# Side-by-side 16-bit one-hots and ranks from column counts in a four-layer graph network kernel

## The chip, the cores and the metric

One core of a Trainium2 chip runs the whole program. The metric is the time on the device in microseconds (us), the median of three runs. The engines are PE (matrix products; its weight loads are listed as PEld), DVE (vector), ACT (scalar, activations), POOL (GpSimd) and SP (which here only issues transfers).

## What is computed

Four graph layers over 6250 nodes with 256 features and 106250 edges, each followed by a sum with its input and a layer norm. The edges are sorted by destination; every undirected edge is there in both directions, and every node has a loop.

```python
edge_index = jnp.stack([src, dst])
x = _layernorm(x + _L0_gnn_ref(x, edge_index, weight, attn_l, attn_r))   # 4-head attention on two rows
x = _layernorm(x + _L1_gnn_ref(x, W, edge_index))                 # segment_sum of h[src] * norm
x = _layernorm(x + _L2_gnn_ref(x, edge_index, w, W1, b1, W2, b2))  # two weighted passes, relu
x = _layernorm(x + _L3_gnn_ref(x, W, edge_index))                 # segment_sum over src of h[dst]
```

A layer is a product with a weight matrix and then a sum over edges of scaled rows of the source node into the destination node.

## The kernel before

**Tiling.** Nodes are 49 blocks of 128 (`NBK`); the feature row of a node lies along one partition. The edges of a destination block fill at most 18 columns (`NC`) of 128, called chunks: 49 x 18 = 882 in all (`NK`). For each chunk POOL gathers the 128 source rows from a table in memory into one of seven tiles `G` (L2062, an indirect transfer; the tile is free when the matmul seven chunks earlier is done, L2061), DVE writes a one-hot of the destination within the block (`M`, L1266, from `dlo`), and PE multiplies both and sums into one bank (L1968).

**Stages.** A first stage does layer 0. Pass 1 (882 chunks) sums the edges of layer 1. Passes 2 and 3 sum those of layer 2, but there only 522 and 486 chunks are gathered; the other blocks are dense products with prepared matrices of edge weights (`AW`, L1927). Layer 4 at the end (L1941, L1999) is dense throughout, with prepared matrices of edge counts (`AT`). Layer 4's degrees are counted in pass 2 with trains of one-hots on DVE (`degrees`, L1286 and L1288).

**What is built behind pass 1.** The matrices `AT` and `AW` are made block by block while pass 1 runs, in spare time of the engines. `build_steps` gives each step a due chunk, 17 chunks (`PITCH`) per block, and `aggregate` on every engine runs its steps of chunk k after its own part of chunk k; within a chunk the steps of earlier blocks come first. Each engine's queue is in order, with semaphores between them. For a block i, in the order of `BORDER`:
- `cellhot` (DVE, L1321 to L1326): `OH`, for each edge a one-hot over 26 places of the pair of source blocks it comes from (a "cell"), 26 x 18 per partition.
- `rank` (PE, L1849 to L1861), in three parts: how many earlier edges share the cell. One matmul with a strictly lower triangle counts earlier partitions of the same column, and 17 matmuls with `onesb` add each column to all later ones.
- `pick`, `pack`, `over`, `less`, `slots` (DVE, L1327 to L1347): read the rank of each edge from bank `PR`, 0 to 127 within a place (an overflow place takes the rest), into `slots`.
- `load` (DVE, L1348): `OHP` = `OH` times the payload of the edge (source within the pair, destination, and for the 22 weighted blocks three pieces of the weight). This is one TENSOR_TENSOR (L1356), with another for weighted blocks (L1355).
- `place` (DVE, L1357): `S`, for each of the 18 columns a one-hot of the slot, one TENSOR_SCALAR of 128 elements each. `permute` (PE, L1862): 18 matmuls of `S` and `OHP` put every edge's payload in its slot. `cells` (ACT, L1625) copies the bank to `clf` (32 bit) and `clb` (16 bit).
- `pairhot` (DVE, L1362), 13 batches of two places a block, 637 in all: `doh`, the one-hot of the destination, one TENSOR_TENSOR for two places with the two values side by side in the last dimension (L1373); `soh`, the one-hot of the source among 256, one TENSOR_SCALAR a place (L1375); for the 286 batches of weighted blocks `wdoh`, `doh` times two weight pieces (L1379). `third` (ACT) writes the third piece.
- `pair` and `weigh` (PE, L1868 to L1893) multiply the one-hots into banks that ACT copies out (`keep`, `keepw`) and SP stores.

The lines that matter most on DVE and PE:

```python
# pairhot, L1373 to L1376
done(e.tensor_tensor(doh[n_ % NB][:, :, 0:g], irepD[:, :, 0:g], value(1, P), ALU.is_equal), ("doh", n_))
for q in range(g):
    done(e.tensor_scalar(soh[n_ % NB][:, q, :], iob[:, :], clf[j][:, j0 + q:j0 + q + 1], None, ALU.is_equal), ("pairhot", n_))
# place, L1361
done(e.tensor_scalar(S[:, c, :], iob[:, 0:P], slots[:, b, c:c + 1], None, ALU.is_equal), ("place", i, c))
```

## Time and profile before

| | |
|---|---|
| median of 3 runs | 3349.37 us (3339.74 to 3351.67) |
| the profiled execution | 3360.17 us, span 3358.4 us |
| granted PE clock, mean | 0.979 |
| PE / PEld / DVE / ACT / POOL busy | 3159.1 / 2556.9 / 2313.6 / 1722.8 / 2046.4 us |
| DMA | 692 MB, mean 206 GB/s |
| pass 1, first to last gather begun | 230.7 to 1413.3 us |
| passes 2 and 3, PE L1970 | 1436.4 to 2803.9 us |
| layer 4, PE L1941 and L1999 | 2782.5 to 3349.9 us |

A row of a group reads: line, engine, operation, tile written <- tiles read, shapes, count | busy us, mean ns of one | idle time in front of them and what ended it. A row of a timeline reads: start, duration, engine, line, operation, and idle time before it. Durations on one engine overlap a little, since an instruction begins before the one in front has ended; the distance from start to start is what one costs in a full queue. "Issue" is time in which an engine waited for nothing that the profile shows.

### The profile page before, as it was taken

The numbers are of one execution on the slowest core, as the hardware profiler recorded it, in microseconds if no ns is written. First come the engines' busy times: TensorE is split into PE (matmuls) and PEld (weight loads), VectorE is DVE, ScalarE is ACT, GpSimd is POOL, SyncE is SP. The second block draws the span as 40 slices with busy tenths as digits, with TensorE's granted clock in tenths as the row PEclk, the third lists the DMA queues.
The fourth block names the chain that finished last, engine by engine and source line by source line (L and its number), as shares of the span: only waits on it lengthen the run. The fifth ranks groups of instructions, "written<-read, shape, count | busy, mean of one in ns | idle before, by whom it ended". The sixth has DMA issues, their size and how long they took to land.

```text
span 3358.4 us, 58810 instructions
## 1 busy us (share of the span) xinstructions
PE 3159.1 (94%) x18605; PEld 2556.9 (76%) x18605; DVE 2313.6 (69%) x9060; ACT 1722.8 (51%) x4557; POOL 2046.4 (61%) x2015
## 2 busy tenths in 40 slices
PE   6789999999999999899999999799999998999999
PEld 5666777767767767678878888688888886888887
DVE  5657998998999889667777777466666664323323
ACT  3554767767767767534444444344444443232232
POOL 6627777777777777677777777577777772000000
PEclk9889999999999999999999999899999999999999
DMA  6256878778878778666666666676666666444443
GB/s 198 76 178 190 252 239 251 249 235 255 253 237 258 245 228 257 213 200 198 204 195 203 203 200 203 226 216 212 213 213 211 213 201 230 149 140 154 166 166 116
DMA packets 335272, 692.21 MB, mean 206 GB/s; under 512 B 63028, under 2 KB 180496, under 8 KB 334062
## 3 DMA queue, kind: packets, MB, share of 16 engines
q1 hardware_dynamic: 237134, 424.16, 37.4%
q0 software_dynamic: 95888, 262.38, 27.9%
q8 instruction: 154, 2.52, 0.3%
q10 hardware_dynamic: 1936, 1.84, 0.2%
q14 instruction: 160, 1.31, 0.1%
HBM read 497.33 MB, written 190.82 MB: 205 GB/s over the span
## 4 chain that ended last, share of the span: by engine, by line
PE 68%; DVE 12%; DMA 10%; POOL 4%; ACT 3%; issue 3%; SPq 0%; ACTq 0%; DVEq 0%
PE PS L1927 22%; PE PS L1999 15%; DMA G<-T,idx 7%; PE PS L1968 7%; PE PS L1970 6%; PE PS L1891 3%; POOL G L2062 2%; PE PS L1757 2%; PE PS L1867 2%; PE PS L1758 2%; DVE soh L1375 2%; PE PS L1858 2%; PE PS L1879 2%; PE PS L1908 1%; DVE M L1266 1%
## 5 line engine op out<-in xcount | busy, mean ns | idle before, releaser
L2062 POOL DMA_INDIRECT G<-T,idx x1890 | 1925.8, 1019 | 647.5 <-issue 275.4
L1927 PE MATMUL PS<-H,aw 128*128 128x256 f32 x4116 | 1052.0, 381 | 0.4 <-DMA aw<-AW 0.4
L1612 ACT ACTIVATE R<-G,wD 128x256 fp32r<-128x256 f32 x1008 | 508.8, 508 | 714.5 <-PE PS L1970 443.3
L1927 PEld LDWEIGHTS PS<-H,aw 128*128 128x128 f32 x4116 | 770.9, 191 | 110.5 <-DMA aw<-AW 0.8
L1275 DVE SCALAR_TENSOR_TENSOR R<-G,wD,R 128x256 fp32r<-128x256 f32 x1008 | 490.1, 486 | 389.4 <-ACT R L1612 385.2
L1968 PE MATMUL PS<-G,M 128*128 128x257 f32 x1764 | 572.5, 408 | 82.3 <-DMA G<-T,idx 32.5
L1970 PE MATMUL PS<-R,Mr 128*128 128x512 f32 x1008 | 583.6, 580 | 31.3 <-DVE R L1275 29.2
L1999 PE MATMUL PS<-HH,cr 128*128 128x512 f32 x2205 | 501.5, 389 | 0.3 <-DVE cr L1453 0.2
L1999 PEld LDWEIGHTS PS<-HH,cr 128*128 128x128 f32 x2205 | 413.3, 188 | 88.3 <-DVE cr L1453 2.6
L1655 ACT CAST atp<-PS 128x512 bf16<-128x512 f32 x588 | 336.5, 572 | 180.8 <-PE PS L1879 174.7
L1968 PEld LDWEIGHTS PS<-G,M 128*128 128x128 f32 x1764 | 297.9, 198 | 160.1 <-DVE M L1266 22.1
L1375 DVE TENSOR_SCALAR soh<-iob,clf 128x256 bf16<-128x256 bf16 x1274 | 313.1, 295 | 0.1
L1699 ACT CAST cr<-br 128x3584 fp32r<-128x3584 bf16 (+1 forms) x42 | 125.1, 2977 | 347.4 <-PE PS L1999 299.5
L1268 DVE TENSOR_SCALAR Mr<-iot,dlo 128x128 fp32r<-128x128 f32 x1008 | 301.5, 301 | 0.0
L1453 DVE CAST cr<-br 128x3584 fp32r<-128x3584 bf16 (+1 forms) x42 | 81.1, 1931 | 319.0 <-PE PS L1999 226.0
L1266 DVE TENSOR_SCALAR M<-iot,dlo 128x128 f32<-128x128 f32 x882 | 256.3, 292 | 48.3 <-PE PS L1968 46.3
L1891 PEld LDWEIGHTS PS<-wdoh,soh 128*128 128x128 bf16 x3432 | 225.9, 96 | 69.9 <-ACT wdoh L1643 14.6
L1879 PE MATMUL PS<-soh,doh 128*128 128x256 bf16 x1225 | 272.7, 273 | 4.0 <-ACT awp L1662 3.0
L1891 PE MATMUL PS<-wdoh,soh 128*128 128x128 bf16 x3432 | 264.7, 219 | 4.2 <-ACT atp L1655 2.4
L1970 PEld LDWEIGHTS PS<-R,Mr 128*128 128x128 f32 x1008 | 193.2, 192 | 77.4 <-DVE R L1275 49.9
L1867 PE MATMUL PS<-OHP,S 128*128 128x52 bf16 (+1 forms) x882 | 248.5, 321 | 2.0 <-DVE S L1361 2.0
L1361 DVE TENSOR_SCALAR S<-iob,slots 128x128 bf16<-128x128 bf16 x882 | 216.6, 268 | 0.0
(231 smaller groups left out, 3908.5 us busy)
## 6 DMA issues: line engine op xcount, KB each, us to landing
aw<-AW SPq DMA_DIRECT2D x294, 448.0 KB
AT<-atp SPq DMA_DIRECT2D x539, 128.0 KB
br<-AT SPq DMA_DIRECT2D x77, 896.0 KB, 4.9
AW<-awp SPq DMA_DIRECT2D x264, 256.0 KB
G<-T,idx POOLq DMA_INDIRECT x1890
AT<-atf SPq DMA_DIRECT2D x49, 256.0 KB
T<-H SPq DMA_DIRECT2D x96, 128.0 KB
cr<-AT SPq DMA_DIRECT2D x7, 1024.0 KB, 4.8
```

The source lines that it names most:

```text
L1275: done(e.scalar_tensor_tensor(out=both[:, D:2 * D], in0=G[slot][:, 0:D], scalar=wD[:, b, c:c + 1], in1=both[:, 0:D].bitcast(F32), op0=ALU. ...
L1375: done(e.tensor_scalar(soh[n_ % NB][:, q, :], iob[:, :], clf[j][:, j0 + q:j0 + q + 1], None, ALU.is_equal), ("pairhot", n_))
L1612: e.activation(R[m % NR][:, 0:D], G[slot][:, 0:D], ACT.Copy, scale=wD[:, k // NC, k % NC:k % NC + 1]).then_inc(s_rw, 1)
L1655: e.copy(atp[n_ % 4][:, 0:wid], fill_bank(*step)[:, 0:wid]).then_inc(s_ar, 1)
L1867: e.matmul(PC[:, 0:q_ * NPOS], S[:, c, :], OHP[:, 0:q_, :, c], start=c == 0, stop=c == NC - 1).then_inc(s_pm, 1)
L1879: ins = e.matmul(ps, d_, s_, start=j != own + 1, stop=True)
L1891: ins = e.matmul(ps[:, h * P:(h + 1) * P], soh[n_ % NB][:, q, h * P:(h + 1) * P], wdoh[n_ % NB][:, t, :, q], start=j != own + 1 and h == 0 ...
L1927: ins = e.matmul(ps, aw[n_ % NAW][:, s_ % 7, :], H[:, s_, :], start=s_ == 0, stop=s_ == NBK - 1)
L1968: e.matmul(ps, M[m % NM][:, :], G[slot][:, 0:D + 1], start=c == 0, stop=c == NC - 1).then_inc(s_mm, 1)
L1970: e.matmul(ps, Mr[m % NM][:, :], R[m % NR][:, :], start=c == 0, stop=c == NC - 1).then_inc(s_mm, 1)
L1999: ins = e.matmul(SET[g % 2][s % 4][:, :], cr[(j + 1) % 2][:, bb, (s % 4) * P:(s % 4 + 1) * P], HH[:, :, b, :], start=b == 0, stop=b == NBK ...
L2062: e.indirect_dma_start(G[slot][:, 0:D], None, TAB[p][0:N, :], bass.IndirectOffsetOnAxis(ap=idx[:, k // NC, k % NC:k % NC + 1], axis=0)).th ...
```

## The change

- `soh` becomes `[P, D, CB]`: both places' values side by side in the last dimension, written by one TENSOR_TENSOR comparison with `irepD` (now 256 long) and `clb`. PE reads `soh` with a step of two. `iob` and `clf` go; the source payload is one greater, since `irepD` counts from 1.
- `S` becomes `[P, 9, P, 2]`: two columns by one TENSOR_TENSOR, from `slots`, now 16 bit and counted from 1 (thresholds 128.5; the triangle holds the diagonal too). `place` is a step for even columns only.
- Ranks: four small matmuls (`totals`) count the edges of each cell in each column, ACT copies the counts (`counted`), and `rank` is one triangle matmul and four matmuls of the counts, spread over all rows, with `prefix`, which is 1 where a column of the same cell comes earlier. `rank` stands three chunks after `totals`, at chunk 4 of the block; it was at chunks 1 to 3.
- A few DVE instructions at the start make `prefix`, and one adds 1 to the payload.

```diff
-        T_ += [(k + 1 + j, ("rank", i, j)) for j in range(3)]
+        T_ += [(k + 1, ("totals", i)), (k + 4, ("rank", i))]
+        S_.append((k + 2, ("totals", i)))
...
-            V_.append((k - 1 + c * 14 // NC, ("place", i, c)))
+            if c % 2 == 0:
+                V_.append((k - 1 + c * 14 // NC, ("place", i, c)))
...
+TG = [slice(0, 7), slice(7, 14), slice(14, 20), slice(20, 26)]
...
+            done(e.tensor_copy(pi[0][:, :], pid[:, :]), "pr0")
...
+            done(e.scalar_tensor_tensor(out=prefix[:, :], in0=iot[:, 0:7 * NC], scalar=row18[:, 0:1], in1=prefix[:, :],
+                                        op0=ALU.is_lt, op1=ALU.mult), "prefix")
...
+            done(e.tensor_scalar(pay2[:, :, 0, :], pay2[:, :, 0, :], 1.0, None, ALU.add), "pay0")
...
-                    w.wait_ge(s_pm, NC * (i - 1) + c + 1)
-                    done(e.tensor_scalar(S[:, c, :], iob[:, 0:P], slots[:, b, c:c + 1], None, ALU.is_equal), ("place", i, c))
+                    w.wait_ge(s_pm, NC * (i - 1) + c + 2)
+                    done(e.tensor_tensor(S[:, c // 2, :, :], irepD[:, 0:P, :], slots[:, b, c:c + 2].unsqueeze(1).to_broadcast([P, P, 2]),
+                                         ALU.is_equal), ("place", i, c))
...
-                    done(e.tensor_tensor(doh[n_ % NB][:, :, 0:g], irepD[:, :, 0:g], value(1, P), ALU.is_equal), ("doh", n_))
-                    for q in range(g):
-                        done(e.tensor_scalar(soh[n_ % NB][:, q, :], iob[:, :], clf[j][:, j0 + q:j0 + q + 1], None, ALU.is_equal),
-                             ("pairhot", n_))
+                    done(e.tensor_tensor(doh[n_ % NB][:, :, 0:g], irepD[:, 0:P, 0:g], value(1, P), ALU.is_equal), ("doh", n_))
+                    done(e.tensor_tensor(soh[n_ % NB][:, :, 0:g], irepD[:, :, 0:g], value(0, D), ALU.is_equal), ("pairhot", n_))
...
+                elif step[0] == "totals":
+                    i = step[1]
+                    w.wait_ge(s_tc, i + 1)
+                    w.wait_ge(s_rk, i - 1)
+                    m_ = (TG[0].stop - TG[0].start) * NC, (TG[2].stop - TG[2].start) * NC
+                    for t in range(2):
+                        ins = e.copy(counted[i % 2][0:m_[t], 2 * t:2 * t + 2], PR[0:m_[t], NPOS * NC + 2 * t:NPOS * NC + 2 * t + 2])
+                    ins.then_inc(s_te, 1)
...
-                    e.copy(clf[i % 2][:, :], PC[:, 0:NPOS])
...
-                if kind == "rank":
-                    O_, part = OH[i % 2], step[2]
+                if kind == "totals":
+                    O_ = OH[i % 2]
                     w.wait_ge(s_v, at["cellhot", i])
                     if i:
                         w.wait_ge(s_v, at["pick", i - 1])
-                    R = PR[:, 0:NPOS * NC].rearrange("p (t c) -> p t c", c=NC)
-                    if part == 0:
-                        e.matmul(PR[:, 0:NPOS * NC], lowerb[:, :], O_[:, :, :], start=True, stop=False)
-                    for c in range(6 * part, min(6 * part + 6, NC - 1)):
-                        ins = e.matmul(R[:, :, c + 1:NC], onesb[:, :], O_[:, :, c:c + 1].to_broadcast([P, NPOS, NC - 1 - c]),
-                                       start=False, stop=c == NC - 2)
-                    if part == 2:
-                        ins.then_inc(s_rk, 1)
+                    for t, g in enumerate(TG):
+                        m_ = (g.stop - g.start) * NC
+                        ins = e.matmul(PR[0:m_, NPOS * NC + t:NPOS * NC + t + 1], O_[:, g, :].rearrange("p t c -> p (t c)"), onesb[:, 0:1],
+                                       start=True, stop=True)
+                    ins.then_inc(s_tc, 1)
+                elif kind == "rank":
+                    O_ = OH[i % 2]
+                    w.wait_ge(s_v, at["prefix"])
+                    w.wait_ge(s_te, i + 1)
+                    e.matmul(PR[:, 0:NPOS * NC], lowerb[:, :], O_[:, :, :], start=True, stop=False)
+                    for t, g in enumerate(TG):
+                        m_ = (g.stop - g.start) * NC
+                        ins = e.matmul(PR[:, g.start * NC:g.stop * NC], counted[i % 2][0:m_, t:t + 1].to_broadcast([m_, P]),
+                                       prefix[0:m_, 0:m_], start=False, stop=t == len(TG) - 1)
+                    ins.then_inc(s_rk, 1)
...
-            io(iob[:, :], [[1, D]])
-            io(irepD[:, :, :], [[1, P], [0, CB]], base=1)
+            io(irepD[:, :, :], [[1, D], [0, CB]], base=1)
```

## Rows read from the trace of the kernel before

**Rows 1.** Busy us (x count) in pass 1: PE, PEld, DVE, ACT, POOL.
```profile
233.50:1419.00 1185.50, 1099.82 (x8571) 831.91 (x8572) 1035.08 (x4999) 810.73 (x2682) 902.46 (x880) 0.98 0.77 239
```

**Rows 2.** The one group of POOL in pass 1.
```profile
L2062 POOL DMA_INDIRECT G<-T,idx x882 | 904.6, 1026 | 290.1 <-issue 189.6 <-PE PS L1968 89.3 <-DMA T<-H 11.2
```

**Rows 3.** Timeline of POOL, a plain stretch: start, duration, line, idle before.
```profile
623.89 0.95 POOL L2062 DMA_INDIRECT G<-T,idx  x1 [0.30 <-issue]
```

**Rows 4.** L2062 in pass 1: duration ns minimum, median, maximum.
```profile
L2062 POOL DMA_INDIRECT G<-T,idx x882: 940/949/2367, 230.7 to 1413.3; - x177
```

**Rows 5.** Timeline of POOL and DVE at a degree train of pass 2.
```profile
1511.32 0.89 DVE L1286 TENSOR_TENSOR big<-irep,lof 128x256 bf16<-128x256 bf16 x4
...
1511.53 1.77 POOL L2062 DMA_INDIRECT G<-T,idx  x1 [0.30 <-DVE R L1275]
...
1512.12 0.36 DVE L1288 TENSOR_TENSOR big<-irep,hi 128x392 bf16<-128x392 bf16 x1
...
1512.40 0.28 DVE L1268 TENSOR_SCALAR Mr<-iot,dlo 128x128 fp32r<-128x128 f32 x1
```

**Rows 6.** The same view at a long gather of pass 1.
```profile
322.33 0.88 DVE L1355 TENSOR_TENSOR OHP<-payw,OH 128x1404 bf16<-128x1404 bf16 x1
...
322.61 1.98 POOL L2062 DMA_INDIRECT G<-T,idx  x1 [0.30 <-issue]
...
323.13 0.63 DVE L1356 TENSOR_TENSOR OHP<-pay,OH 128x936 bf16<-128x936 bf16 x1
```

**Rows 7.** The same view at a gather that a train doesn't stretch.
```profile
1504.27 0.89 DVE L1286 TENSOR_TENSOR big<-irep,lof 128x256 bf16<-128x256 bf16 x4
...
1505.01 0.96 POOL L2062 DMA_INDIRECT G<-T,idx  x1 [0.30 <-DVE big L1286]
```

**Rows 8.** A group by shape in pass 1, and busy us of L1858 alone there.
```profile
L1891 PE MATMUL PS<-wdoh,soh 128*128 128x128 bf16 x3432 | 264.7, 219 | 4.2 <-ACT atp L1655 2.4 <-ACT wdoh L1643 1.3
...
233.50:1419.00 1185.50, 118.89 (x833) 77.66 (x833) 0.98 0.77 239
```

**Rows 9.** Timeline of DVE: one weighted batch and a pair of slot one-hots.
```profile
599.83 0.29 DVE L1373 TENSOR_TENSOR doh<-irepD,clb 128x256 bf16<-128x256 bf16 x1
...
600.03 0.49 DVE L1375 TENSOR_SCALAR soh<-iob,clf 128x256 bf16<-128x256 bf16 x2
...
600.43 0.42 DVE L1379 TENSOR_TENSOR wdoh<-doh,clb 128x512 bf16<-128x512 bf16 x1
...
600.76 0.42 DVE L1361 TENSOR_SCALAR S<-iob,slots 128x128 bf16<-128x128 bf16 x2
...
601.09 0.18 DVE L1065 BATCH_NORM_AGGREGATE mv<-st 128x2 f32<-128x6 f32 x1
```

**Rows 10.** Durations (ns minimum/median/maximum) of DVE's one-hots, and the group of `clf`.
```profile
L1373 DVE TENSOR_TENSOR doh<-irepD,clb x637: 272/284/345, 275.6 to 1396.5; 128x256 bf16<-128x256 bf16 x160
...
L1379 DVE TENSOR_TENSOR wdoh<-doh,clb x286: 404/417/456, 298.8 to 1377.2; 128x512 bf16<-128x512 bf16 x143
...
L1375 DVE TENSOR_SCALAR soh<-iob,clf x1274: 267/281/507, 275.8 to 1396.9; 128x256 bf16<-128x256 bf16 x182
...
L1632 ACT COPY clf<-PS 128x26 f32<-128x26 f32 x49 | 8.7, 178 | 2.4 <-PE PS L1867 2.4
```

**Rows 11.** Start-up: waits of POOL before pass 1, first node cast, the cast of pay2.
```profile
POOL X L2051 <- DVE mv L1065: 55.6, 3, 36.0
...
6.89 0.22 DVE L963 CAST dlo<-win 49x128 f32<-49x128 int32 x1 [4.58 <-DMA win<-in_src]
...
L1130 DVE CAST pay<-ti 128x882 bf16<-128x882 int32 x1 | 1.1, 1072 | 0.0
```

**Rows 12.** The last instruction of each degree train of pass 2.
```profile
L1288 DVE TENSOR_TENSOR big<-irep,hi x104: 348/356/366, 1461.9 to 2103.7; 128x392 bf16<-128x392 bf16 x103, 128x343 bf16<-128x343 bf16 x1
```

**Rows 13.** POOL's groups while the degree trains run, and after them.
```profile
L2062 POOL DMA_INDIRECT G<-T,idx x508 | 527.6, 1039 | 154.7 <-DVE Mr L1268 46.3 <-issue 45.3 <-DVE R L1275 32.6
...
L2062 POOL DMA_INDIRECT G<-T,idx x494 | 487.6, 987 | 184.8 <-DVE Mr L1268 62.1 <-issue 39.0 <-DVE R L1275 30.8
```

More of the change, by code:

```diff
@@ L49 @@
 NAW, NR = 4, 3
-FILL_B, FILL_C = 1208, 290
+FILL_B, FILL_C = 1208, 694
+TG = [slice(0, 7), slice(7, 14), slice(14, 20), slice(20, 26)]
 HEAD = (0, 1, 2, 5, 6, 3, 4)
@@ L720, in program @@
         sel, slot0 = sb("sel", [P, NPOS, NC]), sb("slot0", [P, NC])
-        S = sb("S", [P, NC, P], BF16)
-        soh = [sb(f"soh{i}", [P, CB, D], BF16) for i in range(NB)]
+        S = sb("S", [P, HC, P, 2], BF16)
+        soh = [sb(f"soh{i}", [P, D, CB], BF16) for i in range(NB)]
         doh = [sb(f"doh{i}", [P, P, CB], BF16) for i in range(NB)]
@@ L735, in program @@
         sb = tiles(passes)
-        slots = sb("slots", [P, NBK, NC])
+        slots = sb("slots", [P, NBK, NC], BF16)
         clb = [sb(f"clb{i}", [P, 5, NPOS], BF16) for i in range(2)]
-        clf = [sb(f"clf{i}", [P, NPOS]) for i in range(2)]
         clw = [sb(f"clw{i}", [P, NPOS]) for i in range(2)]
@@ L743, in program @@
         lowerb, onesb, identb = (sb(n_, [P, P], BF16) for n_ in ("lowerb", "onesb", "identb"))
+        prefix = sb("prefix", [P, 7 * NC], BF16)
+        counted = [sb(f"counted{i}", [P, len(TG)], BF16) for i in range(2)]
+        row18 = sb("row18", [P, 1])
         fill2 = sb("fill2", [P, FILL_C])
@@ L1130, in vector @@
             done(e.tensor_copy(pay2[:, :, 0, :], ti[:, :, :]), "pay0")
+            after("pay0")
+            done(e.tensor_scalar(pay2[:, :, 0, :], pay2[:, :, 0, :], 1.0, None, ALU.add), "pay0")
             done(e.tensor_scalar(pay2[:, :, 1, :], dlo[:, :, :], 1.0, None, ALU.add), "pay1")
@@ L1339, in behind_ @@
                     after(("pack", i))
-                    done(e.scalar_tensor_tensor(out=OH[j][:, own + 1, :], in0=slot0[:, :], scalar=127.5, in1=OH[j][:, own, :],
+                    done(e.scalar_tensor_tensor(out=OH[j][:, own + 1, :], in0=slot0[:, :], scalar=128.5, in1=OH[j][:, own, :],
                                                 op0=ALU.is_ge, op1=ALU.mult), ("over", i))
@@ L1381, in behind_ @@
                 elif kind == "bad":
-                    after(("place", NBK - 1, NC - 1))
-                    done(e.tensor_scalar(slots[:, :, :], slots[:, :, :], 127.5, 0.0, ALU.is_ge, ALU.add, accum_out=bad[:, :]), "bad")
+                    after(("place", NBK - 1, NC - 2))
+                    done(e.tensor_scalar(slots[:, :, :], slots[:, :, :], 128.5, 0.0, ALU.is_ge, ALU.add, accum_out=bad[:, :]), "bad")
                 elif kind == "pad":
@@ L1864, in behind_ @@
                     q_ = 5 if b >= NBW else 2
-                    w.wait_ge(s_v, max(at["place", i, c], at["load", i]))
+                    w.wait_ge(s_v, max(at["place", i, c - c % 2], at["load", i]))
                     w.wait_ge(s_ce, i)
-                    e.matmul(PC[:, 0:q_ * NPOS], S[:, c, :], OHP[:, 0:q_, :, c], start=c == 0, stop=c == NC - 1).then_inc(s_pm, 1)
+                    e.matmul(PC[:, 0:q_ * NPOS], S[:, c // 2, :, c % 2], OHP[:, 0:q_, :, c], start=c == 0, stop=c == NC - 1).then_inc(s_pm, 1)
                 elif kind == "pair":
@@ L1873, in behind_ @@
                     fill_free(w, "keep", i, pair // 2)
-                    d_, s_ = doh[n_ % NB][:, :, q], soh[n_ % NB][:, q, :]
+                    d_, s_ = doh[n_ % NB][:, :, q], soh[n_ % NB][:, :, q]
                     if j == own:
@@ L1890, in behind_ @@
                         for t in range(3):
-                            ins = e.matmul(ps[:, h * P:(h + 1) * P], soh[n_ % NB][:, q, h * P:(h + 1) * P], wdoh[n_ % NB][:, t, :, q],
+                            ins = e.matmul(ps[:, h * P:(h + 1) * P], soh[n_ % NB][:, h * P:(h + 1) * P, q], wdoh[n_ % NB][:, t, :, q],
                                            start=j != own + 1 and h == 0 and t == 0, stop=t == 2, skip_group_check=True)
```

19 lines of the change are left out of this document (15 added, 4 removed).

## The prediction

> **What bounds the kernel now.** I read the stages first, then who waits in the stage that the change touches, then single instructions of the engine that never rests there. The profiled execution took 3360.2 us (span 3358.4), 10.8 above the median of 3349.4; my sum is made against it and then moved by that difference. All edits but a few start-up ones lie in pass 1, from the first gather at 230.7 us to the last, which ends at 1414.2. In that stage PE is busy 1099.8 of 1185.5 us, DVE 1035.0 and POOL only 902.5 [rows 1], which invites the conclusion that PE or DVE is the bound. The waits say otherwise. POOL issues one gather for each of the 882 chunks, and its idle time in front of them is 290.1 us, of which 264.6 is the same 0.30 us in front of each (it stands under "issue" and mostly also under PE); beyond that lie 25.5 us, 11.2 of them one wait for the table at the start [rows 2]. So POOL truly waits for PE some 14 us in 1184: it walks through the pass at its own pace, 1.03 + 0.30 us a gather, and PE and DVE fill the time between. In the plain stretch every gather takes 0.94 to 0.95 and starts 0.30 after the last [rows 3]; at that pace the pass would take 882 x 1.245 = 1098 us. It takes 1184 because the mean gather is 1026 ns, median 949, longest 2367 [rows 2, 4]: 904.6 - 882 x 0.945 = **71 us of stretched gathers**, plus the 25.5.
>
> What stretches them? The gather at 1511.53 takes 1.77, 0.83 over the floor. Four TENSOR_TENSORs and a fifth had begun 0.21 before it, back to back; DVE passes on to the next kind at 1512.40, and 1511.53 + 0.83 = 1512.36 [rows 5]. The gather at 322.61, 1.98 long, starts inside an OHP multiply that another follows [rows 6]. A gather which begins under a DVE instruction with two SBUF operands waits for it, often for the whole unbroken train. Not always: the one at 1505.01 takes 0.96 under the same kind of train [rows 7].
>
> **The change, part by part.**
> *Ranks.* The 17 `onesb` matmuls and their loads go; the matmul spans they fill are 118.9 us [rows 8]. New are 8 small matmuls a block; at the 0.143 us of a mean one of the old (118.9 / 833) these are 56 us in all. PE gains some 60 us and loses its tightness, but POOL waited only 14 us for it: at most **-14 us**. ACT gets two tiny copies a block and loses `clf` (178 ns each [rows 10]), +9 us on an engine busy 811 of 1185 [rows 1]. The new chain is cellhot, totals on PE, copies on ACT, rank on PE, `pick` on DVE; rank is queued three chunks after totals, so it waits only if ACT lags by more, and behind it stand the aggregation matmuls. Even 1 us a block hides in the seven gather slots: 0.
> *Source one-hots* (637 batches). Two TENSOR_SCALARs, 0.40 us from start to start, become one TENSOR_TENSOR of 128x512, the shape of `wdoh`, 0.33 [rows 9, 10]: -45 us of DVE.
> *Slot one-hots.* 882 TENSOR_SCALARs, 0.33 a pair, become 441 TENSOR_TENSORs like `doh`, 0.20 [rows 9]: -57 us of DVE. The Trainium skill (VectorE: DVE Perf Modes, section The perf-mode tier table) speaks against this edit: 16-bit `tensor_scalar` runs at four elements a cycle, `tensor_tensor` at two; by the same page's cycle formula (section The TRN2 errata), 58 + n/rate, a pair of 256 would cost 254 ns before and 327 after, so DVE would lose 46 us there. This trace has 0.40 and 0.33 for the two, and I go by it. DVE is not what POOL waits for, so both signs are worth nothing in themselves.
> *Strides.* `soh` is now read by PE with a step of two. `wdoh` already is, and streams 128 columns in 219 ns [rows 8]. No row shows a penalty; if one were 0.1 us per `pair` matmul it would be 127 us of PE, against the 60 freed and the idle 86: 0.
> *Waits.* `place` waits for two permutes instead of one, a period of 17 chunks back: 0. `bad` and the io counts: 0.
> *Start-up.* Seven tiny DVE instructions before the node loads, under a 4.6 us idle: 0. One add on `pay2`, bounded by 0.1 and 1.1 us (the cast beside it is 1.07), taken as 1. The longer iota on POOL stands before a wait of 36 us for DVE [rows 11]: 0.
>
> **The term that decides: longer trains under the gathers.** `doh`, `soh`, `wdoh`, `S` used to be TENSOR_TENSOR 0.20, two TENSOR_SCALARs, TENSOR_TENSOR 0.33, TENSOR_SCALARs. The scalar form breaks the train. Now all four are of the two-operand kind and stand back to back. Train lengths: 351 unweighted batches 0.20 + 0.335 = 0.54; 286 weighted 0.87; about half of each with an `S` of 0.20 behind; 120 lone `S`.
> The price comes from the degree trains of pass 2 (104 of 0.80 + 0.28 = 1.08 us [rows 5, 12]). Gathers average 1039 ns while they run and 987 after [rows 13]: excess 527.6 - 508 x 0.945 = 47.5 us against 487.6 - 494 x 0.945 = 20.8, or 42 ns a gather; 508 x 0.042 = 21.4, so the trains cost 26.1 us, 0.25 each. If gathers began at random and always waited to the end, a train of length L would cost L x L / (2 x 1.33) = 0.44; the share is 0.25 / 0.44 = 0.58.
> New: squares 351 x 0.41 + 286 x 0.95 + 120 x 0.04 = 421, / 2.66 x 0.58 = **+92 us**. Old: 637 x 0.04 + 286 x 0.11 = 57, by the same rule **-12**. Of the other 59 us of today's stretching, the OHP multiplies take about 12 (27 blocks of 0.63 alone, 22 of 1.43 together [rows 6]); 47 are left for 3038 TENSOR_SCALARs (882 `M`, 1274 `soh`, 882 `S`), 2156 of which go: **-33**.
> Sum: +92 - 12 - 33 - 14 + 1 = **+34 us**: profiled 3394, median **3383**. Bounds of the decisive term: share 1 gives 159 (-22 for the old), sum +91, and +124 if the scalar forms cost nothing; at the other end trains stretch nothing more, -12 - 33 - 14 + 1 = -58.
>
> **Rivals.**
> *Faster (0.25).* Gathers are stretched by the scalar forms, not by these trains; those go. Sum -33 to -58: 3291 to 3316, or with a third of the train cost about 3330. The Trainium skill (SBUF — State Buffer, section Who interferes with whom) gives just this: instructions in a two-port mode, 16-bit `tensor_scalar` among them, hold GpSimd off, while `tensor_tensor` takes only the pair's read interface and descriptor generation is inferred to need the write one. For it: gathers begun under `soh` and ended under `wdoh` are among the stretched. Against: 1511.53 and 322.61 stretch under pure TENSOR_TENSOR trains [rows 5, 6]; by this the trace disagrees with the inference. It decides if the train share is under 0.3.
> *Same (0.23).* POOL's pace stays: gathers phase-lock to a DVE that now has room and mostly start between trains; stretching stays near 71, only some of the 14 go. 3335 to 3360. For it: 1505.01 [rows 7].
> *Slower is the forecast (0.52)*, one mechanism: place, the gathers of pass 1; price, 92 us; it decides above a share of 0.3.
> *The edit does not do what it says:* the new comparisons at one element a cycle. `doh` has their form and takes 284 ns for 256 [rows 10]; 0.03, within slower.
>
> **How the numbers follow.** A measurement of this kernel tells about 0.5% (17 us) from no change. Likeliest 3383, its own range 3366 to 3440. The 8-in-10 range takes in "same" and the upper part of "faster": 3318 to 3435. Chances: faster 0.25, within 0.5% 0.23, slower 0.52.
>
> **What would show it.** Right: mean pass-1 gather near 1.08 us (before 1.026), the pass some 1215 us, POOL's idle in front of a gather 0.30 nearly everywhere, PE in the pass under 1050 busy, DVE under 960, weighted blocks stretched more than unweighted, passes 2 and 3 unchanged. Wrong: a mean gather at or under 1.03, or PE and DVE waits in front of POOL.

## The result, and the profile after

The changed kernel takes 3392.7 us (median of 4 runs, 3387.7 to 3396.8) against 3348.6 us before in the same comparison: ratio 1.0138, 95% interval 1.012 to 1.0155. It is **slower by 1.4%**. The prediction said 3383, range 3318 to 3435. The profiled execution took 3393.6 us with a span of 3391.8; the forecast for it was 3394. The medians differ by 44.1 us and the two profiled executions by 33.4, since the profiled one of the kernel before (3360.2) lies 11 above its median. All that follows is read from the profiled ones, so some 10 us of the medians' difference are not accounted for.

The head of the page of the changed kernel, its busy times:

```profile
span 3391.8 us, 56954 instructions
PE 3137.7 (93%) x18164; PEld 2521.5 (74%) x18164; DVE 2234.3 (66%) x7990; ACT 1726.0 (51%) x4606; POOL 2092.6 (62%) x2014
```

The page alone says little: only a stage tells where 33 us went. Three windows of the changed kernel follow, each with POOL's gather group: pass 1 from its first to its last gather, then pass 2 while the degree trains run, and after them to the end of pass 3.

```profile
L2096 POOL DMA_INDIRECT G<-T,idx x882 | 950.6, 1078 | 279.7 <-issue 182.3 <-PE PS L2003 86.3 <-DMA T<-H 11.2
L2096 POOL DMA_INDIRECT G<-T,idx x511 | 529.4, 1036 | 156.1 <-DVE Mr L1290 50.2 <-issue 42.5 <-DVE R L1297 32.9
L2096 POOL DMA_INDIRECT G<-T,idx x494 | 488.3, 988 | 183.9 <-DVE Mr L1290 60.3 <-issue 41.4 <-DVE R L1297 30.1
```

The second and third are as before: 1036 against 1039 ns, 988 against 987 [rows 13]. The first is not: the mean gather of pass 1 went from 1026 to 1078 ns [rows 2], and 882 of them are 46.0 us. Idle time ahead of them fell by 10.4. So the pass is 35.7 us longer, 1218.3 from the first gather's start to the last's (229.7 to 1447.9) against 1182.6 (230.7 to 1413.3), and the whole execution 33.4. The gather's extremes in pass 1, from the view of that line, to be set beside [rows 4]:

```profile
L2096 POOL DMA_INDIRECT G<-T,idx x882: 942/950/2975, 229.7 to 1447.9; - x177
```

The waits ahead of it, from the view of waits (columns: total, times, longest):

```profile
POOL G L2096 <- issue: 182.3, 598, 0.3
POOL G L2096 <- PE PS L2003: 86.3, 283, 0.3
POOL G L2096 <- DMA T<-H: 11.2, 1, 11.2
```

The median gather is still 950 ns: a plain gather costs what it did, and some became much longer. Behind the first, not one gather waits over 0.32 us. POOL sets the pace of pass 1 without a rest, and its pace is set by what stretches it.

What the other engines did in pass 1, one row of the table by window (length, then PE, PEld, DVE, ACT, POOL busy, the granted clock, DMA share, GB/s):

```profile
229.70:1449.00 1219.30, 1078.11 (x8117) 796.49 (x8118) 952.13 (x3920) 813.74 (x2730) 950.62 (x882) 0.95 0.74 233
```

VectorE's groups there:

```profile
L1397 DVE TENSOR_TENSOR soh<-irepD,clb 128x512 bf16<-128x512 bf16 x637 | 264.6, 415 | 0.0
L1288 DVE TENSOR_SCALAR M<-iot,dlo 128x128 f32<-128x128 f32 x876 | 252.4, 289 | 92.2 <-PE PS L2003 90.6
L1396 DVE TENSOR_TENSOR doh<-irepD,clb 128x256 bf16<-128x256 bf16 x637 | 181.1, 284 | 63.2 <-PE PS L1926 48.6 <-PE PS L1914 11.1 <-PE PS L1912 1.5
L1383 DVE TENSOR_TENSOR S<-irepD,slots 128x256 bf16<-128x256 bf16 x441 | 124.2, 282 | 0.0
L1400 DVE TENSOR_TENSOR wdoh<-doh,clb 128x512 bf16<-128x512 bf16 x286 | 119.0, 416 | 0.0
```

VectorE was relieved as costed, by 83 us of busy time (1035.1 to 952.1), and spends the relief waiting: 92 us ahead of `M` and 63 ahead of `doh`. It is faster and gets no further.

How a gather is stretched shows in single instructions. A **train** is a row of VectorE instructions without idle time between them, a **seam** the point where one hands over to the next. VectorE's timeline around 783 us in the changed kernel (start, duration):

```profile
782.93 0.28 DVE L1396 TENSOR_TENSOR doh<-irepD,clb 128x256 bf16<-128x256 bf16 x1
783.13 0.41 DVE L1397 TENSOR_TENSOR soh<-irepD,clb 128x512 bf16<-128x512 bf16 x1
783.47 0.41 DVE L1400 TENSOR_TENSOR wdoh<-doh,clb 128x512 bf16<-128x512 bf16 x1
783.81 0.28 DVE L1383 TENSOR_TENSOR S<-irepD,slots 128x256 bf16<-128x256 bf16 x1
784.01 0.98 DVE L1359 TENSOR_REDUCE slot<-sel 128x18 f32<-128x468 f32 x1
```

POOL's timeline there:

```profile
783.00 1.91 POOL L2096 DMA_INDIRECT G<-T,idx  x1 [0.31 <-issue]
```

The gather begins under `doh`, 0.07 us after that was issued, and takes 1.91 us instead of 0.945. The extra 0.965 ends at 783.97, and the train of four ends with `S`, which hands over to the reduction at 784.01.

**A tally of all 882 gathers** makes this a number. For each, s is its start and e = duration - 0.945 us. The tally looks up the VectorE instruction under way at s and the one under way at s + e. If it is the same one, e is put down to that instruction's **own** hold; if it is a later one, to a **seam** that was crossed. (Excesses under 0.04 us, some 2 us in all, are left out. At s, an instruction counts as under way from 0.03 us after its recorded start, so a gather that begins less than that behind a seam is put down to the instruction ahead of it.)

| | stretch, us | own, us (gathers) | seam, us (gathers) |
|---|---|---|---|
| before | 71.1 | 24.8 (219) | 44.3 (124) |
| changed | 117.1 | 29.8 (197) | 85.3 (165) |

Own holds are 5 us more, seams 41. Without the 0.03 us it is 31.3 own and 37.8 seam before, 34.7 and 80.4 changed: 3 us and 43. The split depends on that choice, its change much less. A second count takes the gathers that begin while an instruction runs with another right behind it, and asks whether they are held more than 0.06 us past the handover (before and changed together; "two" is a TENSOR_TENSOR of `doh`, `soh`, `wdoh`, `S` or the load, "one" a TENSOR_SCALAR of `M`, `soh` or `S`):

| running, then next | held past the handover, shifted window | the same, strict window |
|---|---|---|
| one, then two | 158 of 210 | 107 of 225 |
| two, then two | 122 of 237 | 116 of 276 |
| one, then one | 14 of 135 | 2 of 181 |
| two, then one | 9 of 195 | 0 of 227 |
| either, then anything else | 3 of 166 | 0 of 218 |

The strict window is from the recorded start of the running instruction to that of the next. The shifted one, from which the counts of this kind further down come unless they are called strict, is from 0.09 us after the first to 0.06 us after the second, so it also takes in gathers that begin when the next is already under way. Both say the same.

What the *next* instruction is decides: a gather can be held past a handover if the next has two operands, and hardly ever otherwise. That does not mean that one-operand instructions hold nothing. Of the strict gathers that begin at least 0.09 us ahead of a handover to anything but a two-operand instruction, 65 of 70 under `doh` are over 0.04 us longer and 99 of 100 under `wdoh`, but also 44 of 84 under a one-operand `soh`, 10 of 15 under `M` and 7 of 45 under a one-operand `S`; under the other instructions of VectorE it is 3 of 139. Nearly all of these are held to about 0.04 us before the handover and no longer. In the tally 5.2 of the 24.8 us of own holds before come from one-operand forms, 1.5 of the 29.8 in the changed kernel. All this was read from traces; the experiments put the part on the seam to the test.

### The profile page after: what moved, and what is told of

The parts are those of the page before. It is cut to its first block, busy times and chain, and to the rows that moved or that the text cites. A ratio compares the mean times of both kernels' runs of the same rounds, so it can differ in the third digit from the quotient of the medians.

```text
span 3391.8 us, 56954 instructions
## 1 busy us (share of the span) xinstructions
PE 3137.7 (93%) x18164; PEld 2521.5 (74%) x18164; DVE 2234.3 (66%) x7990; ACT 1726.0 (51%) x4606; POOL 2092.6 (62%) x2014
## 4 chain that ended last, share of the span: by engine, by line
PE 65%; DMA 15%; DVE 7%; POOL 6%; issue 3%; ACT 3%; SPq 0%; ACTq 0%; DVEq 0%
PE PS L1962 21%; PE PS L2034 14%; DMA G<-T,idx 13%; PE PS L2003 8%; PE PS L2005 5%; POOL G L2096 5%; PE PS L1926 4%; PE PS L1785 2%; PE PS L1786 2%; PE PS L1902 2%; PE PS L1914 2%; PE PS L1943 1%; PE PS L1976 1%; DVE R L1297 1%; DVE soh L1397 1%
## 5 line engine op out<-in xcount | busy, mean ns | idle before, releaser
L2096 POOL DMA_INDIRECT G<-T,idx x1890 | 1971.3, 1043 | 635.4 <-issue 267.2
L2003 PE MATMUL PS<-G,M 128*128 128x257 f32 x1764 | 598.0, 424 | 141.5 <-DMA G<-T,idx 83.1
L2005 PE MATMUL PS<-R,Mr 128*128 128x512 f32 x1008 | 582.2, 579 | 32.3 <-DVE R L1297 30.4
L1914 PE MATMUL PS<-soh,doh 128*128 128x256 bf16 x1225 | 280.8, 281 | 0.6 <-ACT awp L1690 0.6
L1926 PEld LDWEIGHTS PS<-wdoh,soh 128*128 128x128 bf16 x3432 | 229.4, 98 | 66.8 <-ACT wdoh L1671 10.1
L1926 PE MATMUL PS<-wdoh,soh 128*128 128x128 bf16 x3432 | 265.7, 220 | 2.5 <-ACT atp L1683 1.2
L1397 DVE TENSOR_TENSOR soh<-irepD,clb 128x512 bf16<-128x512 bf16 x637 | 264.6, 415 | 0.0
L1396 DVE TENSOR_TENSOR doh<-irepD,clb 128x256 bf16<-128x256 bf16 x637 | 181.1, 284 | 63.2 <-PE PS L1926 48.6
```

What stands on the lines that cost most here:

```text
L1914: ins = e.matmul(ps, d_, s_, start=j != own + 1, stop=True)
L1926: ins = e.matmul(ps[:, h * P:(h + 1) * P], soh[n_ % NB][:, h * P:(h + 1) * P, q], wdoh[n_ % NB][:, t, :, q], start=j != own + 1 and h == 0 ...
L2003: e.matmul(ps, M[m % NM][:, :], G[slot][:, 0:D + 1], start=c == 0, stop=c == NC - 1).then_inc(s_mm, 1)
L2005: e.matmul(ps, Mr[m % NM][:, :], R[m % NR][:, :], start=c == 0, stop=c == NC - 1).then_inc(s_mm, 1)
L2096: e.indirect_dma_start(G[slot][:, 0:D], None, TAB[p][0:N, :], bass.IndirectOffsetOnAxis(ap=idx[:, k // NC, k % NC:k % NC + 1], axis=0)).th ...
```

## The experiments

The table has all runs; the sections take them in turn. Time and ratio are from several executions; pass 1, stretch and the last column are from one profiled execution of each kernel, so how much they scatter is not known, and differences of a few us in them say little. Pass 1 is from the first to the last gather's start; stretch is POOL's busy time there over 882 x 0.945 us. The ratio is to runs of the kernel before on the same chip, whose median lay between 3348.6 and 3356.3 us, so ratios are compared, not times.

| kernel | median, us | ratio (95%) | pass 1 | stretch | own / seam |
|---|---|---|---|---|---|
| before | 3348.6 | 1 | 1182.6 | 71.1 | 24.8 / 44.3 |
| changed | 3392.7 | 1.0138 (1.012 to 1.0155) | 1218.3 | 117.1 | 29.8 / 85.3 |
| ranks alone | 3338.0 | 0.9952 (0.9936 to 0.9969) | 1172.5 | 69.8 | 26.5 / 41.1 |
| one-hots alone | 3396.6 | 1.0119 (1.0099 to 1.0139) | 1231.7 | 122.1 | 30.1 / 90.3 |
| changed, `S` by scalar | 3370.6 | 1.0043 (1.003 to 1.0055) | 1204.2 | 100.6 | 34.0 / 65.0 |
| changed, `soh` by scalar | 3354.0 | 0.9996 (0.9983 to 1.0009) | 1180.2 | 73.8 | 19.3 / 52.5 |
| one-operand gaps behind `doh`, `soh` | 3344.3 | 0.9983 (0.9968 to 0.9998) | 1173.3 | 70.8 | 33.6 / 35.4 |
| the same with two-operand gaps | 3356.7 | 1.0008 (0.9989 to 1.0026) | 1184.7 | 81.8 | 31.2 / 48.0 |
| as many ahead of `M` instead | 3419.6 | 1.0211 (1.0186 to 1.0235) | 1250.2 | 146.3 | 21.8 / 122.7 |
| changed, gaps at every seam | 3328.0 | 0.9931 (0.9914 to 0.9947) | 1160.7 | 56.3 | 30.4 / 24.1 |
| before, gaps | 3333.3 | 0.9949 (0.9931 to 0.9968) | 1163.7 | 40.3 | 29.7 / 8.5 |
| ranks alone, gaps | 3314.2 | 0.9895 (0.9871 to 0.9919) | 1141.5 | 37.1 | 26.1 / 8.8 |
| `soh` by scalar, gaps | 3313.4 | 0.9886 (0.9868 to 0.9904) | 1148.0 | 45.2 | 29.1 / 14.3 |

One sum makes up every row: 881 x (0.945 + 0.30) = 1096.8 us, plus the stretch, plus the idle time beyond 0.30 between gathers (14.6 before, 4.3 changed, 26.5 before with gaps, 5.6 to 12.8 in the others) is the pass. For the changed kernel 1096.8 + 117.1 + 4.3 = 1218.2. It adds up by definition; what it says is where the differences lie, in the stretch, and how little is left for waits.

### Ranks alone

Slots and sources are again 32-bit values, `S` and `soh` written a column at a time:

```diff
-                    done(e.tensor_tensor(S[:, c // 2, :, :], irepD[:, 0:P, :], slots[:, b, c:c + 2]....to_broadcast([P, P, 2]),
-                                         ALU.is_equal), ("place", i, c))
+                    done(e.tensor_scalar(S[:, c, :], iob[:, 0:P], slots[:, b, c:c + 1], None, ALU.is_equal), ("place", i, c))
...
-                    done(e.tensor_tensor(soh[n_ % NB][:, :, 0:g], irepD[:, :, 0:g], value(0, D), ALU.is_equal), ("pairhot", n_))
+                    for q in range(g):
+                        done(e.tensor_scalar(soh[n_ % NB][:, q, :], iob[:, :], clf[j][:, j0 + q:j0 + q + 1], None, ALU.is_equal),
+                             ("pairhot", n_))
```

Expected:

> The changed kernel's ranks alone: slots and the cells' sources are again 32-bit values and their one-hots (S, soh) are again written one column at a time by tensor_scalar. Trains theory (what the change costs is that VectorE's two-input instructions now stand back to back and hold up POOL's gathers for as long as they stream): the gathers' stretch over their 945 ns floor is back near 71 us (117 in the changed kernel), POOL's mean gather near 1.02 to 1.03 us, the pass from first to last gather 1170 to 1185 us, and the time 3330 to 3347 us (before 3349). Rival, ranks (the new chain of totals, a copy on ScalarE and a prefix on TensorE comes later than the old matmuls did): the loss stays, 3380 to 3395 us, and the stretch of the changed kernel has to come from elsewhere. Rival, no part alone (the loss is the sum of TensorE's lower clock and longer loads in both): near 3370 us.

Measured: ratio 0.9952, faster by 0.5%. Its gathers in pass 1:

```profile
L2100 POOL DMA_INDIRECT G<-T,idx x882 | 903.2, 1024 | 281.9 <-issue 195.3 <-PE PS L2006 74.8 <-DMA T<-H 11.8
```

Its row by window:

```profile
228.10:1401.70 1173.60, 1050.17 (x8117) 788.18 (x8118) 1031.05 (x4999) 814.69 (x2779) 903.24 (x882) 0.97 0.78 242
```

The stretch is that of before and the idle time beyond 0.30 fell from 14.6 to 5.9: the new ranks are a gain by themselves. The pass is 10.1 us shorter, in which PE is busy 1050.2 us; the ratio stands for some 16 us (11 to 21). Time, stretch and pass are as the trains theory expected.

### One-hots alone

The other half: the paired one-hots with the ranks of the kernel before.

```diff
-        T_ += [(k + 1, ("totals", i)), (k + 4, ("rank", i))]
-        S_.append((k + 2, ("totals", i)))
+        T_ += [(k + 1 + j, ("rank", i, j)) for j in range(3)]
```

> The changed kernel's paired one-hots with the ranks of the kernel before (one triangular matmul and 17 matmuls over broadcast columns of edges). Trains theory: stretch 112 to 125 us, mean gather 1.07 to 1.09 us, time 3390 to 3407 us: the ranks gave back at most some 14 us and their absence costs that much. Rival, ranks: with the old ranks the time is back at 3345 to 3355 us, and the stretch with it. Rival, no part alone: near 3370 us.

Measured: 1.0119, with a mean gather of 1083 ns:

```profile
L2088 POOL DMA_INDIRECT G<-T,idx x882 | 955.6, 1083 | 288.2 <-issue 189.3 <-PE PS L1995 87.8 <-DMA T<-H 11.1
```

The whole loss is in the one-hots, and in the stretch. The pass is 13.4 us longer than the changed kernel's, as the ranks' gain is gone; the median is only 4 us above, with overlapping intervals. Together the two runs settle which half costs.

### `S` by scalar, `soh` by scalar

The changed kernel with one of the two put back, by the lines shown above.

> The changed kernel with the slots' one-hots S put back: 32-bit slots, 18 tensor_scalar instructions a block of edges instead of 9 tensor_tensor. The same values are computed. Trains theory: what the gathers lost under S and under chains that ran into S goes (by the tally of the changed kernel's trace some 45 to 60 us of the 117 us end in a chain that holds an S), part of it comes back as chains that now end elsewhere: stretch 75 to 95 us and time 3350 to 3375 us, although VectorE is busy some 50 us longer. Rival, work (what counts is how long VectorE is busy and how late its one-hots are): slower than the changed kernel, 3395 to 3420 us. Rival, ranks: unchanged, 3388 to 3398 us.

> The changed kernel with the sources' one-hots soh put back: 32-bit values copied by ScalarE, one tensor_scalar for each column of a batch instead of one tensor_tensor for the two. S stays paired. Trains theory: soh no longer lies between doh and wdoh, so those chains end at doh: stretch 80 to 105 us, time 3355 to 3385 us, with VectorE busy some 45 us longer. Rival, work: 3395 to 3415 us, since more of VectorE's time stands before the pair's matmuls. Rival, ranks: unchanged, 3388 to 3398 us.

Measured: 1.0043 and 0.9996. VectorE's two groups and the gathers in the run with `S` by scalar:

```profile
L1396 DVE TENSOR_TENSOR soh<-irepD,clb 128x512 bf16<-128x512 bf16 x637 | 266.8, 419 | 0.0
L1383 DVE TENSOR_SCALAR S<-iob,slots 128x128 bf16<-128x128 bf16 x882 | 216.6, 267 | 0.0
L2096 POOL DMA_INDIRECT G<-T,idx x882 | 934.1, 1059 | 282.4 <-issue 196.8 <-PE PS L2002 74.2 <-DMA T<-H 11.3
```

The same of the run with `soh` by scalar:

```profile
L1400 DVE TENSOR_SCALAR soh<-iob,clf 128x256 bf16<-128x256 bf16 x1274 | 314.1, 296 | 0.1
L1385 DVE TENSOR_TENSOR S<-irepD,slots 128x256 bf16<-128x256 bf16 x441 | 126.0, 286 | 0.0
L2102 POOL DMA_INDIRECT G<-T,idx x882 | 907.3, 1029 | 285.3 <-issue 191.1 <-PE PS L2008 82.8 <-DMA T<-H 11.4
```

Both give VectorE more to do (1003 and 981 us busy in the pass against 952) and both are faster than the changed kernel, which rules out that VectorE's work sets the time here. The two edits aren't alike. Against the ranks alone (stretch 69.8), pairing only `S` adds 4 us, pairing only `soh` 31, pairing both 47. `soh` is the one that joins `doh` to what comes after; the two scalar `soh`s between `doh` and the rest are what kept the trains short. The stretch after putting `S` back is 100.6, above my 75 to 95: chains that had ended in `S` now ended in `soh` or `wdoh`. For `soh` it is 73.8, below my 80 to 105, and the time is 1 us below its range.

### A gap at the seams, of either kind

All work stays as in the changed kernel, and a one-element instruction (a "tiny") is put behind `doh`, behind `soh` and ahead of `S` (1715 in pass 1). Its result is read by nobody.

```diff
+            def between():
+                turn[0] += 1
+                t_ = turn[0] % 24
+                done(e.tensor_scalar(tiny[0][:, t_:t_ + 1], tiny[1][:, :], 1.0, None, ALU.mult))
...
                     w.wait_ge(s_pm, NC * (i - 1) + c + 2)
+                    between()
                     done(e.tensor_tensor(S[:, c // 2, :, :], ...
...
                     done(e.tensor_tensor(doh[n_ % NB][:, :, 0:g], ...
+                    between()
                     done(e.tensor_tensor(soh[n_ % NB][:, :, 0:g], ...
+                    between()
```

> The changed kernel with a one-element instruction of one operand (tensor_scalar, its result read by nobody) behind every doh, behind every soh and ahead of every S, so that no two of these tensor_tensor instructions follow one another directly; all of the tensor_tensor work is still there. Trains theory in its form 'it is the back-to-back seam that carries a hold over': a gather that starts under one of them is held only to its end, not to the end of the next; stretch 65 to 90 us instead of 117, time 3345 to 3375 us although some 1715 instructions are added to VectorE. Rival, sum (a gather is held by each two-input instruction that runs, wherever it stands): stretch stays at 110 to 125 us and the time 3390 to 3410 us. Rival, work (VectorE's busy time and the added instructions delay the one-hots): 3410 to 3450 us.

The second of the pair uses `done(e.tensor_tensor(tiny[0][:, t_:t_ + 1], tiny[1][:, :], tiny[2][:, :], ALU.mult))` instead.

> The same as between_one in number and place, but the one-element instruction is itself a tensor_tensor with both operands in SBUF. If the kind of the instruction between is what breaks a chain, the chains stay whole here: stretch 105 to 130 us and 3390 to 3420 us. If any further instruction, however short, gives the gather its turn, it ends as between_one does (within 8 us). If the added instructions cost time by themselves, both are slower than the changed kernel.

Measured: 0.9983 and 1.0008, stretch 70.8 and 81.8 us. A train in the timeline of the first:

```profile
378.31 0.28 DVE L1406 TENSOR_TENSOR doh<-irepD,clb 128x256 bf16<-128x256 bf16 x1
378.51 0.15 DVE L1320 TENSOR_SCALAR tiny<-tiny 128x1 f32<-128x1 f32 x1
378.57 0.42 DVE L1408 TENSOR_TENSOR soh<-irepD,clb 128x512 bf16<-128x512 bf16 x1
378.91 0.21 DVE L1320 TENSOR_SCALAR tiny<-tiny 128x1 f32<-128x1 f32 x2
379.03 0.28 DVE L1393 TENSOR_TENSOR S<-irepD,slots 128x256 bf16<-128x256 bf16 x1
```

POOL's timeline there:

```profile
378.64 1.17 POOL L2108 DMA_INDIRECT G<-T,idx  x1 [0.30 <-issue]
```

The groups of its tinies and its gathers in pass 1:

```profile
L1320 DVE TENSOR_SCALAR tiny<-tiny 128x1 f32<-128x1 f32 x1715 | 232.8, 142 | 0.0
L2108 POOL DMA_INDIRECT G<-T,idx x882 | 904.3, 1025 | 281.1 <-issue 186.7 <-PE PS L2015 83.2 <-DMA T<-H 11.2
```

The gathers of the run with two-operand gaps:

```profile
L2108 POOL DMA_INDIRECT G<-T,idx x882 | 915.3, 1038 | 281.5 <-issue 193.5 <-PE PS L2015 76.8 <-DMA T<-H 11.1
```

The gather begins 0.07 us after `soh` was issued, just as the one at 783.00 did after `doh`, and with a `tiny` and an `S` to come. It is held 0.23 us, until `soh` hands over, and no longer. A tiny costs VectorE 0.06 us from start to start (378.51 to 378.57), and 1715 of them paid for themselves: the rivals "sum" and "work" are out. So is most of my idea that the kind of the tiny matters. The second run fits neither of its expectations: its stretch is far under 105 us, but its time is 12 us above the first's, not within 8. With two operands the tiny breaks the chain too: of gathers that began under a two-operand instruction with a tiny next, 8 of 282 were held past the handover in the first run and 9 of 268 in the second. Both lose to chains that begin under `M`, behind which no tiny stands (by the tally `M` to `doh` is 13.0 us of the stretch in the first run, 20.9 in the second). The second also loses more to gathers that begin under the tiny itself: by the strict count 46 of 87 with a two-operand instruction next were held past the handover, against 12 of 59. Why stays open in both cases.

### The same instructions where no seam is

```diff
                 w.wait_ge(s_mm, m - NM + 1)
+                if p == 1 and k < NK - 60:
+                    between()
+                    between()
```

> The changed kernel with nearly as many one-element tensor_scalars as in the run with gaps behind doh and soh (1644 against 1715), but all of them two by two ahead of M, the destination one-hot of a chunk, and so at none of the seams between doh, soh, wdoh and S. Seam theory: the trains stay whole, stretch 105 to 125 us (117.1 in the changed kernel, 70.8 with the gaps at the seams) and time 3385 to 3400 us. Rival, any gap (more instruction boundaries or idle time on VectorE let gathers through, wherever they stand): stretch 70 to 95 us and 3345 to 3375 us. Rival, work: above 3400 us.

Measured: 1.0211, the slowest kernel of all, stretch 146.3 us. Its gathers and tinies in pass 1:

```profile
L2108 POOL DMA_INDIRECT G<-T,idx x882 | 979.8, 1111 | 282.6 <-issue 194.7 <-PE PS L2015 76.7 <-DMA T<-H 11.2
L1323 DVE TENSOR_SCALAR tiny<-tiny 128x1 f32<-128x1 f32 x1636 | 164.1, 140 | 51.4 <-PE PS L2015 50.4
```

That any gap does is refuted; the trains stay whole and so does their price. But the seam theory missed the size, by 21 us of stretch over its range and 20 us of time. By its time alone the run falls to the rival "work" (above 3400 us). Against that rival: VectorE is no busier than in the run with the gaps at the seams (1043.5 against 1040.6 us), and the pass, 77 us longer, is so by the gathers' stretch, with 7.1 us of idle time beyond 0.30; the seams' part alone is 122.7 us. `M` to `S` went from 17.8 us in the changed kernel to 36.8. A gather's excess depends on where in a train it starts, and tinies ahead of `M` shift that; this is an argument, and no run tests it.

### Gaps at every seam: before, changed, and mixed

Three gaps in the kernel before, ahead of `doh` (behind `M`), ahead of `wdoh`, and ahead of the second instruction of the load; the same three with the new ranks; those and `S` with `soh` by scalar; and one ahead of every `doh`, `soh`, `wdoh`, `S` and second load in the changed kernel.

```diff
+                    between()
                     done(e.tensor_tensor(doh[n_ % NB][:, :, 0:g], ...
...
                         after(("doh", n_))
+                        between()
                         done(e.tensor_tensor(wdoh[n_ % NB][:, 0:2, :, 0:g], ...
...
+                    between()
                     done(e.tensor_tensor(OHP[:, 0:2, :, :], *spread_(pay2[:, b, :, :], 2), ALU.mult), ("load", i))
```

> The kernel before with nothing changed but a one-element tensor_scalar ahead of every doh, every wdoh and the second instruction of the load: the same three places as in the run with the ranks and the gaps. If the seams are what costs and the ranks' gain adds to it, stretch 36 to 50 us instead of 71.1 and time 3320 to 3334 us, ratio 0.990 to 0.995. If the gain of that run came mostly from an interplay with the ranks, 3340 to 3350 us. If added instructions cost: above 3355 us.

> The kernel of the run with the ranks alone (3338 us, stretch 69.8 us), with a one-element tensor_scalar ahead of every doh, of every wdoh and of the second instruction of the edges' load, where its trace shows a gather that began under the instruction ahead held to the end of the tensor_tensor behind it (soh to wdoh 13.1 us, M to doh 10.4, load to load 10.7, soh to load 5.9). If the seam carries the hold, stretch 45 to 58 us and time 3318 to 3332 us. If not, the added instructions cost nothing or some us: 3335 to 3350 us, stretch unchanged at 65 to 75 us.

> The changed kernel (paired one-hots, new ranks) with a one-element tensor_scalar ahead of every doh, soh, wdoh, S and the second instruction of the load. Seam theory: all that is left is each instruction's own hold; the paired soh holds longer than a single tensor_scalar did, so stretch 45 to 62 us and time 3320 to 3340 us, between the run with gaps behind doh and soh (3344 us, of which some 13 us lay from M to doh and 12 in the load) and the ranks with gaps (3314). If the paired forms have no cost but the seam, it equals the ranks with gaps within 5 us. If VectorE's time now counts, above 3344 us.

> soh by tensor_scalar, S paired, new ranks, with the one-element instruction ahead of every doh, wdoh, S and the second instruction of the load. Seam theory: stretch 37 to 50 us, time 3310 to 3328 us, as the ranks with gaps (3314 us), since VectorE is busy 50 us less in S and no seam is left. If an S of two operands holds gathers by itself more than two of one operand: 3325 to 3340 us. This is also the candidate for the best kernel.

Measured, in this order: 0.9949, 0.9895, 0.9931, 0.9886. The first, third and fourth fall in the ranges of the seam theory; the ranks with gaps gained more than expected, with a stretch of 37.1 us against 45 to 58 and 3314.2 us against 3318 to 3332. The gathers in pass 1 of the kernel before with gaps:

```profile
L2074 POOL DMA_INDIRECT G<-T,idx x882 | 873.8, 991 | 302.2 <-issue 186.9 <-PE PS L1980 104.0 <-DMA T<-H 11.3
```

Of the ranks alone with gaps:

```profile
L2112 POOL DMA_INDIRECT G<-T,idx x882 | 870.6, 987 | 283.5 <-issue 190.2 <-PE PS L2018 81.6 <-DMA T<-H 11.7
```

The row by window of the same:

```profile
231.90:1374.60 1142.70, 1048.58 (x8117) 783.06 (x8118) 1079.48 (x5971) 813.20 (x2779) 870.60 (x882) 0.97 0.79 248
```

The gathers of the changed kernel with gaps:

```profile
L2110 POOL DMA_INDIRECT G<-T,idx x882 | 889.8, 1009 | 283.8 <-issue 193.2 <-PE PS L2017 78.7 <-DMA T<-H 11.8
```

And of `soh` by scalar with gaps:

```profile
L2115 POOL DMA_INDIRECT G<-T,idx x882 | 878.7, 996 | 281.5 <-issue 194.1 <-PE PS L2021 76.2 <-DMA T<-H 11.2
```

Three gaps in the kernel before take the seams' part from 44.3 to 8.5 us and make it 0.5% faster. What is gained falls partly into idle time, which rises from 14.6 to 26.5: here POOL waits for PE (104.0 us against 89.3, of which 0.30 in front of each gather is the floor). With the new ranks that wait is gone too, and the two together give 1.05%: the ranks are worth 10.1 us of the pass without the gaps, 22.2 with them (1163.7 to 1141.5). The changed kernel with gaps keeps all its paired one-hots and beats the kernel before by 0.7%. It does not reach the ranks with gaps within 5 us, so the paired forms have a cost beside the seam. By the tally 24.1 us of seams are left in it, but most of that is the 0.03 us of the tally's rule: without it 10.0 us are seams and 44.5 own holds, against 2.8 and 32.1 in the ranks with gaps. Over the four runs of this section 323 gathers began strictly between the start of a tiny and that of the two-operand instruction behind it, and 54 were held past the handover, 52 of them among the 93 that began in the last 0.03 us. Of those that began 0.03 to 0.06 us after the start of the two-operand instruction, all 92 were held. The two best differ by less than their intervals. Both beat both kernels.

## Why the prediction was right, and where it was not

- **The bound** (POOL walks through pass 1 at its own pace): shown. Over thirteen kernels the pass runs from 1141 to 1250 us and the stretch from 37 to 146, while the idle time beyond 0.30 stays between 4 and 27; PE's busy time in the pass runs from 1043 to 1124 and VectorE's from 952 to 1084, neither in the order of the times.
- **Ranks, at most -14 us**: the pass is 10.1 us shorter in the run with the ranks alone, and idle beyond 0.30 fell from 14.6 to 4.3 us in the changed kernel. Right in place; in size too by the traces, while the ratio of that run stands for 11 to 21 us.
- **Source and slot one-hots, -45 and -57 us of VectorE, worth nothing in themselves**: VectorE's busy time fell by 83; from start to start 102 had been costed. Worth nothing: the two runs with one form put back have more VectorE time and less total. By the cycle formula of the Trainium skill (VectorE: DVE Perf Modes, section The TRN2 errata) a pair of 256 would have been dearer in the new form. The trace does not agree: 0.34 us from `soh` to `wdoh` at 783.13, where the two scalar forms take 0.40 [rows 9].
- **Strides**: L1926, which reads `soh` with a step of two, takes 220 ns against 219 [rows 8]. Right.
- **The trains, +92 - 12 - 33 = +47 us of stretch**: measured +46.0. The mechanism was right and so was the sum; its three terms were not separated by any run, the share of 0.58 that scaled them came from another pass, and the last term has the wrong cause, so that they meet the measured sum so closely is in part luck. The experiments give the better form: the seams' part rose by 41.0 us and the own holds by 5.0. The -33 for scalar forms that go was put down to holds of their own. The tally has only 5.2 us of such holds in the kernel before and 1.5 in the changed one, 3.7 less. The other cause that the counts show lies at the seams: a gather that began under a scalar form was often held past the handover by the two-operand instruction behind it (158 of 210; strict 107 of 225), and with another scalar form behind it rarely (14 of 135; strict 2 of 181).
- **Rival faster** (trains don't stretch): refuted. The inference of the Trainium skill that it rested on (SBUF — State Buffer, section Who interferes with whom) does not carry over to this gather. Here `tensor_tensor` holds gathers both alone and in trains: breaking nothing but the seams gave 46 us of stretch back. The gather also reads its row numbers from `idx`, a tile in SBUF, and no run tells that read from the writing of descriptors; which of the two is held is not shown. One part of the rival is true: the scalar forms hold gathers too, but for 5.2 us in all. **Rival same** (phase-lock keeps the stretch near 71): refuted by 117.1.
- **PE under 1050 us busy in the pass**: missed, 1078. The ranks alone reach 1050, so the matmuls went as costed, but in the changed kernel the rest grew. Its matmul of the gathered rows in the changed kernel:

```profile
L2003 PE MATMUL PS<-G,M 128*128 128x257 f32 x1755 | 595.0, 423 | 141.5 <-DMA G<-T,idx 83.1 <-DVE doh L1396 13.2 <-DVE M L1288 12.3
```

  The same with the ranks alone:

```profile
L2006 PE MATMUL PS<-G,M 128*128 128x257 f32 x1755 | 581.1, 415 | 120.5 <-DMA G<-T,idx 63.0 <-DVE soh L1398 10.0 <-DVE S L1384 9.0
```

  PE waits 20 us more for gathers and each matmul is 8 ns longer, at a granted clock of 0.95 in the pass against 0.97. It is late because the gathers are, not the other way round: behind the first, no gather waits over 0.32 us for PE.
- **Weighted blocks stretched more than unweighted**: missed. The excess is 136 ns a gather in weighted and 141 in unweighted blocks (102 and 67 before). The squares of train lengths said otherwise, since a `wdoh` makes a train of 0.54 one of 0.87. What I left out is that `M` begins the chain in both, and that a weighted block had had a seam (`soh` to `wdoh`) already.
- **The other signs**: mean gather near 1.08 (1.078), pass near 1215 (1218.3), VectorE under 960 (952), no wait of POOL over 0.32 behind the first, passes 2 and 3 unchanged. Right.

## What to carry to other kernels

When an engine issues indirect gathers back to back, look at its mean against its median duration: the difference is time that another engine takes from it, and no busy share shows it. Fusing two short one-operand instructions into one two-operand instruction can cost more than it saves if it closes the last gap in a train; order such instructions so that something of another form stands between, or put a one-element instruction at the seam (0.06 us each). Count what the engine that sets the pace gets, not what the edited engine saves.

## What the runs showed of the hardware

- An indirect gather that begins while a two-operand instruction on SBUF tiles runs on VectorE is held to about its end (65 of 70 under `doh`, 99 of 100 under `wdoh`), and can be held on by the next in line if that has two operands too: 122 of 237, strict 116 of 276. A gather that begins under a one-operand instruction can be held by a two-operand one behind it as well (158 of 210, strict 107 of 225). With anything else behind it, it is hardly ever held past the handover (26 of 496, strict 2 of 626).
- One-operand instructions hold gathers to their own end too, though less often: 44 of 84 under the 16-bit `soh`, 10 of 15 under the 32-bit `M`.
- A one-element instruction at the seam is enough, even one of two operands (8 of 282 and 9 of 268 held past it), though it keeps VectorE for only 0.06 to 0.07 us. A gather that begins in the last 0.03 us before the two-operand instruction behind the tiny was held in 52 of 93 cases, one that begins earlier under the tiny in 2 of 230.
- The same instructions at another place made the kernel some 0.7% slower (ratio 1.0211 against 1.0138), with VectorE no busier than in the run with the gaps at the seams (0.9983). The position of the gathers against the trains matters by tens of us, and I could not forecast it. Whether the seams of the degree trains in pass 2 would pay as well was not tried.
